# Splitting the Q, K and V projection into three accumulation groups in an attention and feed-forward kernel

## The reference: what is computed

```python
x = x + layernorm(attn(layernorm(x), w_qkv, w_out))
x = x + layernorm(ffn(layernorm(x), W_r, W_k, W_v, mu_r, mu_k))

def attn(x, w_qkv, w_out):              # 16 heads of 64 channels, window 512
    q, k, v = split(x @ w_qkv, 3)
    q = q * cos + rotate_half(q) * sin  # rotary embedding, k likewise
    k = k * cos + rotate_half(k) * sin
    s = q @ k.T / 8                     # causal, and at most 511 tokens back
    return softmax(s) @ v @ w_out

def ffn(x, ...):                        # xr, xk: x mixed with its predecessor
    return sigmoid(xr @ W_r.T) * (relu(xk @ W_k.T) ** 2 @ W_v.T)
```

## Time and profile before

| what | value |
|---|---|
| time, median of 3 runs | 3056.25 us (3055.04 to 3057.26) |
| the profiled execution | 3057.37 us |
| its span on the slowest core (core 7) | 3055.8 us |
| spans of the 8 cores | 3045.4 to 3055.8 us |
| TensorE (PE) matmuls, busy | 1278.5 us (42%), 7048 instructions |
| VectorE (DVE), busy | 1043.0 us (34%), 1791 instructions |
| ScalarE (ACT), busy | 474.8 us (16%) |
| GpSimd (POOL), busy | 77.4 us (3%) |
| mean granted TensorE clock, core 7 | 0.596 of full speed |

### The profile page before, as it was taken

How to read it: one execution, slowest core, us unless ns; L and a number is a source line. 1 busy time by engine, 2 the same in 40 slices (tenths; PEclk the granted TensorE clock), 3 DMA queues, 4 the chain that set the end, 5 groups by cost and what they waited for, 6 DMA issues and landing times. The chain is left out here.

```text
span 3055.8 us, 20808 instructions; the slowest of 8 cores (3045.4 to 3055.8 us)
## 1 busy us (share of the span) xinstructions
PE 1278.5 (42%) x7048; PEld 734.8 (24%) x7048; DVE 1043.0 (34%) x1791; ACT 474.8 (16%) x955; POOL 77.4 (3%) x37
## 2 busy tenths in 40 slices
PE   0254344434434444344453444444444034343434
PEld 0122222232322323223232232322323011111111
DVE  2232323232332322323223232232322254555454
ACT  0012111111111111111111111111111021112121
POOL 0000000000000000000000000000000001010000
PEclk9975555555555555555555555555555557576767
DMA  6200000000000000000000000000000500001000
GB/s 187 86 0 1 14 14 0 14 1 14 1 14 14 1 14 1 14 14 1 14 1 14 14 1 14 0 14 14 0 14 1 174 33 29 34 28 35 34 29 28
DMA packets 19814, 70.92 MB, mean 23 GB/s; under 512 B 2944, under 2 KB 2944, under 8 KB 19584
## 3 DMA queue, kind: packets, MB, share of 16 engines
q1 hardware_dynamic: 19712, 69.59, 7.0%
HBM read 52.28 MB, written 17.30 MB: 23 GB/s over the span
## 5 line engine op out<-in xcount | busy, mean ns | idle before, releaser
L539 PE MATMUL PS<-sb_ident,Pb 128*128 128x128 bf16 x1344 | 164.9, 308 | 572.0 <-DVE Pb L519 535.4
L484 ACT ACTIVATE Pb<-PS,sb_consts 128x640 bf16<-128x640 f32 x256 | 224.2, 880 | 994.0 <-DVE PS L460 994.0
L539 PEld LDWEIGHTS PS<-sb_ident,Pb 128*128 128x128 bf16 x1344 | 132.7, 141 | 604.2 <-issue 604.2
L281 PE MATMUL PS<-wqkv_b,xlt 128*128 128x512 bf16 x960 | 251.9, 430 | 23.1 <-DVE xlt L261 23.1
L578 PE MATMUL PS<-PTb,v_ring 128*64 128x128 bf16 x1344 | 167.7, 311 | 176.5 <-DVE PTb L552 176.5
L608 PE MATMUL PS<-wout_b,oT 64*128 64x512 bf16 x544 | 234.7, 629 | 13.6 <-DVE oT L591 13.6
L254 PE MATMUL PS<-sb_ident,xln 128*128 128x128 bf16 x160 | 20.2, 307 | 409.7 <-DVE xln L240 409.7
L578 PEld LDWEIGHTS PS<-PTb,v_ring 128*64 128x64 bf16 x1344 | 139.0, 169 | 208.7 <-issue 208.7
L552 DVE COPY PTb<-PS 128x1280 bf16<-128x1280 bf16 (+1 forms) x136 | 111.0, 816 | 199.2 <-PE PS L539 199.2
L429 PE MATMUL PS<-kT_ring,qTp 128*128 128x128 bf16 x1072 | 153.1, 310 | 20.2 <-DVE kT_ring L381 20.2
L281 PEld LDWEIGHTS PS<-wqkv_b,xlt 128*128 128x128 bf16 x960 | 102.3, 108 | 168.1 <-issue 83.2
(11 more groups left out here) (96 smaller groups left out, 1488.0 us busy)
## 6 DMA issues: line engine op xcount, KB each, us to landing
stag<-wqkv SPq DMA_DIRECT2D x24, 512.0 KB, 4.5
xb<-x_ext SPq DMA_DIRECT2D x20, 512.0 KB, 4.1
x2t<-x2spill SPq DMA_DIRECT2D x20, 512.0 KB, 3.3
x2spill<-x2s SPq DMA_DIRECT2D x17, 512.0 KB, 2.9
out<-outb SPq DMA_DIRECT2D x16, 512.0 KB, 2.6
stag<-wout SPq DMA_DIRECT2D x16, 256.0 KB, 3.5
stag<-wr SPq DMA_DIRECT2D x8, 512.0 KB, 4.0
stag<-wk SPq DMA_DIRECT2D x8, 512.0 KB, 4.2
```

The lines of the kernel that those rows point to most:

```text
L281: r = eng.matmul(PSf[:, w * 1024 + half * 512: w * 1024 + half * 512 + 512], lhs, wqkv_b[:, c * 3072 + w * 1024 + half * 512: c * 3072 + w ...
L484: r = eng.activation(Pb[:, poff:poff + 640], PSf[:, hoff:hoff + 640], AF.Exp, bias=CB, scale=CS, accum_out=sums[:, srot + h:srot + h + 1])
L539: r = eng.transpose(PSb[:, pdst + t * 128:pdst + (t + 1) * 128], Pb[:, poff + cc:poff + cc + 128], ident[:])
```

## The change

The function that emitted the 48 matmuls of a burst in one piece (`qkv_fn`) becomes `qkv_part`, which emits the 16 matmuls of one of the three projections, over all 8 slices of the contraction. It is called three times, for Q, for K and for V, and each call raises TensorE's semaphore at its end. The V part keeps the name `("qkv", j)`, so that ScalarE's copy of V waits for the end of all 48 matmuls as before. VectorE's rotary embedding of Q now waits for the Q part alone, and that of K for the K part. In the first three rounds, which have no Q on VectorE, its one wait is for the K part.

```diff
--- before.py
+++ after.py
@@ -271,20 +271,21 @@
                     if ("ropeK", j - 1, "d") in M:
                         S.w("tensor", "sDVE", M[("ropeK", j - 1, "d")]["sDVE"])
 
-                def qkv_fn(jj):
+                def qkv_part(jj, w):
                     def f(eng):
                         r = None
                         for c in range(8):
                             lhs = xlt[:, c * 128:(c + 1) * 128]
                             for half in range(2):
-                                for w in range(3):
-                                    r = eng.matmul(PSf[:, w * 1024 + half * 512: w * 1024 + half * 512 + 512],
-                                                   lhs,
-                                                   wqkv_b[:, c * 3072 + w * 1024 + half * 512: c * 3072 + w * 1024 + half * 512 + 512],
-                                                   start=(c == 0), stop=(c == 7))
+                                r = eng.matmul(PSf[:, w * 1024 + half * 512: w * 1024 + half * 512 + 512],
+                                               lhs,
+                                               wqkv_b[:, c * 3072 + w * 1024 + half * 512: c * 3072 + w * 1024 + half * 512 + 512],
+                                               start=(c == 0), stop=(c == 7))
                         return r
                     return f
-                M[("qkv", j)] = S.e("tensor", qkv_fn(j), ("sPE",), banks={0, 1, 2, 3, 4, 5})
+                M[("qkvq", j)] = S.e("tensor", qkv_part(j, 0), ("sPE",), banks={0, 1})
+                M[("qkvk", j)] = S.e("tensor", qkv_part(j, 1), ("sPE",), banks={2, 3})
+                M[("qkv", j)] = S.e("tensor", qkv_part(j, 2), ("sPE",), banks={4, 5})
 
                 S.w("scalar", "sPE", M[("qkv", j)]["sPE"])
                 M[("vev", j)] = S.e("scalar",
@@ -305,7 +306,10 @@
                         return eng.tensor_tensor(tB, swap, sin_ap, ALU.mult)
                     return f
 
-                S.w("vector", "sPE", M[("qkv", j)]["sPE"])
+                if j >= QT0 and upto != 21:
+                    S.w("vector", "sPE", M[("qkvq", j)]["sPE"])
+                else:
+                    S.w("vector", "sPE", M[("qkvk", j)]["sPE"])
                 if upto == 21:
                     M[("ropeK", j, "g")] = M[("qkv", j)]
                     M[("ktev", j)] = M[("c1", j)]
```

## The result

| | before | after |
|---|---|---|
| median of 8 runs | 3058.3 us | 2930.1 us (2926.6 to 2940.9) |
| ratio, with its 95% interval | | 0.9581 (0.9565 to 0.9596) |
| the profiled execution | 3057.4 us | 2940.9 us |
| its span | 3055.8 us (core 7) | 2939.3 us (core 0) |

What follows compares the result with a forecast made beforehand. It took phase 1 to be bound by one chain of steps per tile, not a busy engine. Terms 112.2 + 10.4 + 7 = 129.6 us off the profiled 3057.4 gave 2927.8, put at 2927 for the median; range 2912 to 2948.

Steps and rivals of the forecast that it cites:

- The chain: In phase 1 no engine is near full; time taken off a tile's chain of steps comes off once per tile.
- The new order: TensorE's 48 matmuls of a burst, reordered from six banks in turn to two, were costed at nothing.
- The waits: VectorE starts embedding Q 6.79 us and K 3.22 us before T, the end of a tile's burst of matmuls.
- The added wait: VectorE's wait for the K part before embedding K costs nothing, that part having been done for 0.2 us.
- The scores: In tiles with attention they start 3.1 to 3.2 us behind the burst's end in place of 9.74.
- The term for the 17 tiles: In tiles with attention the scores start 6.6 us earlier, times 17 = 112.2 us.
- the three tiles without attention: Only K is embedded there, starting 3.45 us earlier, times 3 = 10.4 us.
- The first scores: Ten small matmuls at the start of attention may run at TensorE's high clock: 7 us taken, from 0 to 8.5.
- The clock that does not rise: Rival: TensorE's clock stays low in bursts of the new order, 20.5 us each; 3098 us, chance 0.04.
- VectorE slowed beside matmuls: Rival: VectorE's embedding operations take 1.24 us more each inside the burst; gain 63 us, time 2994, chance 0.04.

Runs made afterwards that it cites:

- the run again: The changed kernel without an edit, for a second profile and a ratio against the kernel before: 2931.6 us, ratio 0.9585.

## Why the prediction was right

The chain. The prediction read the tile as one chain, in which time taken off comes off once per tile. The early x load, worth the same 106 to 107 us in both kernels, shows it from another place of the chain, and so do the early statistics (109 us in the trace).

The new order, costed at nothing: 3062.5 against 3062.9 us with the order alone.

The waits. VectorE was to start at T - 6.79 and T - 3.22, and did at T - 6.80 and T - 3.23. `knat` was to end at T + 0.43 and ended at T + 0.42. The added wait was to cost nothing; there is no idle time ahead of K.

The scores were put at T + 3.1 to T + 3.2 and start at T + 3.02. The transposes of Q end at T + 0.44 (950.67 + 0.61) and not at T + 0.6. They overlap the last matmul by 0.17 us and not by 0.1, and with my own 0.61 and 0.1 it should have been T + 0.5. The term for the 17 tiles was 112.2 us. By the means of the 17 tiles (medians of the 8 cores) the scores go from T + 9.78 to T + 3.02, and 6.76 x 17 = 114.9. For the three tiles without attention it was 10.4; from the first burst to the fourth there are 72.5 us before and 62.2 after, 10.3 less.

The first scores. I took 7 us, a choice between 0 and 8.5. In the second profile of the changed kernel all 136 sets of first scores, 17 on each of 8 cores, start at the high level of the clock. In the first profile 120 do, 14 start at 0.81 and 2 at the low level. In the kernel before and in the two with one early wait all 136 start at the low one. From the first score to the mask this saves 0.52 us in the tile above, but from the first score to GpSimd's addition at the tile's end only 0.39 (93.56 to 93.17 us, medians of the cores), and 0.39 x 17 = 6.6. The direction was reasoned, that the size came out as close was luck. The rule on transposes of the Trainium skill that I weighed there ("TensorE: Matmul & The Clock Gate", Part 4) pointed to a smaller term. In the runs the scores came at T + 3.0 at the high clock, and at T + 6.2 and T + 6.3 at the low one. Whether the transposes held the clock or the shorter time was enough is not shown.

Together 114.9 + 10.3 + 6.6 = 131.8. The median span of the 8 cores is 3050.6 us in the profile before and 2919.1 in the second profile after, 131.5 less. The medians of the slowest core differ by 128 in the first comparison and by 131 in the one with the run again. The 3 us between them lie in how the slowest of 8 cores comes out, which neither the forecast nor an experiment went into.

The rivals. The clock that does not rise: no burst in the new order shows it. VectorE slowed beside matmuls: 1.22 to 1.23 us in every kernel. The row that spoke for it, line 925 with 1.93 us, has another neighbour. In the trace of the kernel before, GpSimd's addition of that time is:

```profile
2519.68 2.35 POOL L1055 TENSOR_TENSOR outb<-x2t,t2b 128x1024 f32<-128x1024 f32 x1 [137.33 <-ACT t2b L1041]
```

It runs to 2522.03, over 1.38 of the 1.93 us from 2520.65. In that trace line 925 takes 0.69 us in the 4 calls with no addition of GpSimd beside them, and 1.64 to 1.99 us in the 12 that share 1.1 to 1.4 us with one. TensorE is busy all through the 4 short ones and idle beside the 12 long ones, so it is not the neighbour that slows them. A look at what else ran would have spared that rival its weight.

## What to carry to other kernels

Where one engine waits for a group of matmuls that fill several independent outputs, put the outputs one behind the other and signal each: the reader starts with the first, and here the new order cost TensorE nothing (ratio 0.9999). The gain is the reader's time as far as it fits under the rest of the group, here 6.9 us of 7.2, and it stops at the first work that needs the last output. In a chain with idle engines, look for every step that could be done a tile ahead: the x load and the statistics gave another 200 us, more than the change itself.

## What the runs showed that I had not expected

TensorE's granted clock had a third value. In the first profile of the changed kernel, 15 of the 80 bursts on cores 0 to 3 took more than 13.6 us, counted from their first weight load. The first two rows are stretches inside bursts of core 0, then comes core 2, and then core 4 (window, length, PE, PEld, DVE, ACT, POOL, PEclk, DMA):

```profile
694.00:702.00 8.00, 8.00 (x32) 3.32 (x31) 7.13 (x6) 0.00 (x0) 0.00 (x0) 0.81 0.00 0
944.00:950.00 6.00, 6.00 (x29) 2.73 (x28) 5.85 (x5) 0.00 (x0) 0.00 (x0) 1.00 0.00 0
...
944.00:950.00 6.00, 3.95 (x35) 2.46 (x33) 3.74 (x5) 1.02 (x1) 0.00 (x0) 0.81 0.01 3
...
694.00:697.00 3.00, 3.00 (x15) 1.37 (x14) 2.93 (x4) 0.00 (x0) 0.00 (x0) 1.00 0.00 0
```

The granted clock is the third number from the end of a row: the eighth burst of core 0 ran at 0.81 of 2.4 GHz, with 32 matmuls in 8.00 us, that is 0.25 each in place of 0.216. No burst of cores 4 to 7 was over 13.6 us in that execution, none of any core in the second profile, nor in those of the kernel before and of the order alone. With one more operation on VectorE there were six again, on cores 0 and 1. With the statistics ahead there were six on cores 6 and 7, and with the copy of K on ScalarE as well 14 on cores 4 to 7. The value was in the profile before too, in the second phase, on cores 0, 1, 4 and 5. These rows are core 0 and core 2 there:

```profile
2714.00:2720.00 6.00, 6.00 (x25) 2.46 (x24) 3.08 (x6) 2.18 (x5) 0.00 (x0) 0.81 0.00 0
...
2714.00:2720.00 6.00, 6.00 (x29) 2.74 (x28) 3.05 (x6) 3.33 (x6) 0.14 (x1) 1.00 0.00 0
```

In all five profiles it comes to two neighbouring cores at nearly the same distances from their starts (0 and 1, 2 and 3, 4 and 5, 6 and 7), and the other pair of the same die has it at other distances, in part or throughout, or not at all. The Trainium skill, "TensorE: Matmul & The Clock Gate", Part 1, describes a limit for a whole die at 13/16, which is 0.81, once three of its cores run dense matmuls. The value agrees with the trace. The whole die is not borne out: within 944 to 950 core 0 is at 1.00 and core 2 at 0.81, though the trace does not tell how the starts of the cores lie to each other. What brings it, and why it comes in some executions and not in others of the same kernel, was not tried. It cost the first profile some 9 us in its bursts (258.5 against 249.7).
